# Attention over 1,024 keys and values: one unit of probabilities in eight turned by TensorE, where it was one in four

## What is computed

```python
def _L2_xattn_ref(x, cond, Wq, bq, Wkv, bkv, Wp, bp):
    ...
    q = (x @ Wq + bq).reshape(1, B * N, H, hd)
    kv = (cond @ Wkv + bkv).reshape(1, -1, 2, H, hd)
    ...
    attn = jnp.einsum('bhqd,bhkd->bhqk', q, k)
    attn = jax.nn.softmax(attn.astype(jnp.float32), axis=-1)
    attn = _fq_unsigned(attn, axis=-1)      # s = max/255; round(x/s) clipped to 0..255, times s
    out = jnp.einsum('bhqk,bhkd->bhqd', attn, v)
    out = jnp.transpose(out, (0, 2, 1, 3)).reshape(B, N, C)
    return out @ Wp + bp
```

## Time and profile before

| | us |
|---|---|
| median of three runs | 1028.89 (1026.59 to 1029.68) |
| the profiled execution | 1028.76 |
| its span, first to last instruction | 1027.0 |
| the attention loop, first maximum to the last exponentials (578.65 to 773.75) | 195.1 |
| TensorE, VectorE, ScalarE busy in that stretch | 140.6, 165.2, 173.2 |
| granted TensorE clock over the span, and in that stretch | 0.844, 0.51 |

### The profile page before, as it was taken

How to read it: one execution, slowest core, us unless ns; L and a number is a source line. 1 busy time by engine, 2 the same in 40 slices (tenths; PEclk the granted TensorE clock), 3 DMA queues, 4 the chain that set the end, 5 groups by cost and what they waited for, 6 DMA issues and landing times.

```text
span 1027.0 us, 11627 instructions
## 1 busy us (share of the span) xinstructions
PE 858.3 (84%) x4214; PEld 508.3 (49%) x4214; DVE 728.5 (71%) x958; ACT 461.2 (45%) x695; POOL 166.3 (16%) x251
## 2 busy tenths in 40 slices
PE   5989974589799999989899677677778988879898
PEld 3434652345655555545455333343344656644566
DVE  1776669954558787887668888788884456568767
ACT  2214436731424422212124588899995444622211
POOL 1000000000022442326100261111110100001412
PEclk9899995589889999989899855555558899979999
DMA  8602003000123221340104889967761000000000
GB/s 257 202 1 47 1 0 63 6 3 6 29 37 45 39 37 16 63 56 4 31 16 76 160 156 158 159 124 137 138 128 32 31 0 1 1 1 1 10 11 21
DMA packets 211613, 59.14 MB, mean 58 GB/s; under 512 B 192399, under 2 KB 209893, under 8 KB 211557
## 3 DMA queue, kind: packets, MB, share of 16 engines
q1 hardware_dynamic: 211444, 58.23, 29.2%
q10 hardware_dynamic: 112, 0.17, 0.1%
HBM read 20.62 MB, written 1.05 MB: 21 GB/s over the span
## 4 chain that ended last, share of the span: by engine, by line
PE 51%; DVE 27%; ACT 9%; issue 6%; DMA 5%; POOL 1%; ACTq 1%; DVEq 0%; POOLq 0%
PE ps L950 48%; DMA arena<-xc 4%; DVE arena L2609 4%; ACT xc L1893 2%; ACT arena L1903 1%; DVE arena L2243 1%; DVE arena L2173 1%; PE ps L1081 1%; DVE xc L2415 1%; ACT arena_split L1810 1%; DVE arena L2618 1%; DVE sq L2522 1%; DVE sq L2519 1%; PE ps L472 1%; DVE arena L2157 1%
## 5 line engine op out<-in xcount | busy, mean ns | idle before, releaser
L950 PE MATMUL ps<-arena 128*128 128x16 f16 (+7 forms) x1760 | 268.5, 324 | 62.2 <-ACT xc L1893 27.1
L950 PEld LDWEIGHTS ps<-arena 128*128 128x128 f16 (+4 forms) x1760 | 132.1, 129 | 172.9 <-issue 81.7
L950 PE MATMUL ps<-arena_split 128*128 128x512 f32 (+6 forms) x736 | 197.9, 432 | 18.7 <-DVE arena_split L2065 5.8
L950 PEld LDWEIGHTS ps<-arena_split 128*128 128x128 f32 (+6 forms) x736 | 133.3, 194 | 90.0 <-issue 40.5
L2609 DVE TENSOR_REDUCE arena<-ps 128x1 f32<-128x1024 f32 x128 | 152.4, 1220 | 29.8 <-PE ps L950 28.1
L1893 ACT ACTIVATE xc<-ps,arena 128x1024 int16<-128x1024 f32 x128 | 153.2, 1202 | 21.9 <-POOL arena L908 18.8
L950 PE MATMUL ps<-sq,arena 128*64 128x256 f32 (+3 forms) x256 | 80.9, 515 | 8.1 <-DVE sq L2522 8.1
L908 POOL TENSOR_SCALAR arena<-arena 128x1 f32<-128x1 f32 x128 | 33.8, 264 | 192.9 <-DVE arena L2609 192.6
L857 POOL TENSOR_SCALAR arena<-arena 128x512 f32<-128x512 f32 x12 | 23.1, 1921 | 249.0 <-DVE arena L2437 249.0
L1662 ACT ACTIVATE act_buf<-ps 128x512 f32<-128x512 f32 (+2 forms) x34 | 20.3, 597 | 90.5 <-PE ps L950 90.4
L950 PE MATMUL ps<-mean_w,sq 128*128 128x1 f32 x240 | 34.4, 273 | 21.3 <-ACT sq L1627 21.3
(11 more groups left out here) (291 smaller groups left out, 1322.0 us busy)
## 6 DMA issues: line engine op xcount, KB each, us to landing
arena<-in_L_ffn_w SPq DMA_DIRECT2D x4, 640.0 KB, 6.1
arena_split<-arena_split SPq DMA_DIRECT2D x59, 32.0 KB
arena<-xc SPq DMA_TRANSPOSE x96, 3.3
arena<-in_x SPq DMA_DIRECT2D x1, 1024.0 KB, 6.2
arena<-in_ctx SPq DMA_DIRECT2D x1, 1024.0 KB, 8.7
arena<-in_L_xattn_Wkv SPq DMA_DIRECT2D x2, 512.0 KB, 4.1
arena<-in_L_ffn_gate_w SPq DMA_DIRECT2D x1, 1024.0 KB, 10.0
arena<-in_L_ffn_up_w SPq DMA_DIRECT2D x1, 1024.0 KB, 12.5
```

The source lines that it names most:

```text
L950: return pe.matmul(o, l, r, start=start, stop=stop)
```

## The change

One unit of eight (u % 8 == 7) is turned by TensorE, not two. Unit 3 of each eight becomes a DMA transpose on SP's queue with a semaphore of its own. VectorE copies what TensorE turns; ScalarE's 16 copies (L1903) are gone. The copy waits in the units named change accordingly (u // 8 + 1 in place of u // 4 + 1, unit u-8 in place of u-4 as the previous user of bank 7).

```diff
-        att_copied_dve, att_copied_act = sem("att_copied_dve"), sem("att_copied_act")
-        att_t = {i: sem(f"att_t{i}") for i in range(8) if i % 4 != 3}
+        att_copied = sem("att_copied")
+        att_t = {i: sem(f"att_t{i}") for i in range(7)}
...
         def by_pe(u):
 
-            return u % 4 == 3
-
-        def copied_by_act(u):
-
             return u % 8 == 7
...
         def turned_back(u):
 
             if by_pe(u):
-                return (att_copied_act if copied_by_act(u) else att_copied_dve), u // 8 + 1
+                return att_copied, u // 8 + 1
             return att_t[u % 8], 16 * (u // 8 + 1)
...
             def probs_turned(u):
                 pe.wait_ge(att_exp, u + 1)
-                if u >= 4:
-
-                    pe.wait_ge(*turned_back(u - 4))
+                if u >= 8:
+
+                    pe.wait_ge(*turned_back(u - 8))
...
-            for u in range(UNITS + 4):
-                if u < UNITS:
-                    exponentials(u)
-                if u >= 4 and copied_by_act(u - 4):
-                    probs_copy(u - 4)
+            for u in range(UNITS):
+                exponentials(u)
...
-                if u >= 4 and by_pe(u - 4) and not copied_by_act(u - 4):
+                if u >= 4 and by_pe(u - 4):
                     probs_copy(u - 4)
```

More of the change, by code:

```diff
@@ L625, in probs_read @@
         def probs_read(u):
-            return (att_pe_turned, u // 4 + 1) if by_pe(u) else (att_t[u % 8], 16 * (u // 8 + 1))
+            return (att_pe_turned, u // 8 + 1) if by_pe(u) else (att_t[u % 8], 16 * (u // 8 + 1))
         def turned_back(u):
             if by_pe(u):
-                return (att_copied_act if copied_by_act(u) else att_copied_dve), u // 8 + 1
+                return att_copied, u // 8 + 1
             return att_t[u % 8], 16 * (u // 8 + 1)
@@ L2612, in probs_copy @@
             def probs_copy(u):
-                dve.wait_ge(att_pe_turned, u // 4 + 1)
+                dve.wait_ge(att_pe_turned, u // 8 + 1)
                 if u >= 8:
@@ L2618, in probs_copy @@
                 dve.tensor_copy(att_yt[:, u % 8].rearrange("p a b -> p (a b)"), ps[:, 7, :].bitcast(I16)
-                                ).then_inc(att_copied_dve, 1)
+                                ).then_inc(att_copied, 1)
             def out_copied(h, banks):
```

## The result

| | before | after |
|---|---|---|
| median | 1029.41 us (1026.59 to 1034.89), 12 runs | 1027.06 us (1022.68 to 1028.73), 12 runs |
| ratio | | 0.9967, 95% interval 0.9953 to 0.9981 |
| profiled execution: span | 1027.0 | 1025.6 |
| the exponentials' starts, first to last | 192.2 | 187.4 |
| all outside of that | 834.8 | 838.2 |

The kernel became 0.33% faster, 3.4 us by the ratio, where 9.2 us were forecast. The time lies inside the range, but the gain is a third of the one foretold. So the question is where the other 6 us went.

A forecast was written before the change was run, and what follows sets the result against it. No engine was full; rings of waits with hardly any slack set the attention loop's pace. A gain of 18.3 us, less 2.0 and (8.4 + 2.1 - 3.4), left 9.2: from 1028.76 to 1019.6 us, range 1012.5 to 1028.5.

The forecast's parts named there:

- The copies' 1.29 us a period: Attention loop: without ScalarE's copy, its 0.91 us and the 0.38 behind it fall away every eight units.
- One turn goes, one stays: no gain booked: Attention loop: of TensorE's two turns per eight units one goes, without gain; the remaining one costs what the other did.
- The price of a turn: Attention loop: the remaining TensorE turn, with VectorE's copy, makes two slow steps between exponentials, 1.70 and 1.73 us.
- The quiet period, 10.75: Eight undisturbed units of the attention loop: 10.62 us plus 0.13 for taking out a tile, against 11.90 before.
- The query tiles, 8.4: Four query tiles on SP's queue in the loop delay the units behind them: 2.1 us each, 8.4 in all.
- DMA backlog and slow landings, 2.0 + 2.1: Loop's DMA transposes: 2.0 us for lateness within runs of units, 2.1 for two of four other slow landings.
- The sign that I had named: ScalarE's waits move from the bias to the DMA, concentrated behind the four query tiles, 8 to 10 us in sum.
- Rival 1: DMA in the loop is hidden altogether, only the query tiles cost what they did: 1013.5 us; chance 0.16.
- rival 2: Loop's runs of seven transposes land after about 4.5 us, not 3.3, eating the gain: 1028 us; chance 0.13.
- Rival 3: Loop's exponentials wait for DMA transposes, which become the bound; kernel slower, 1043 us, or 1035 at 4.8 landing; chance 0.09.
- the page's figure: Loop's DMA transposes at 261 GB/s, not 192: a unit passes in 1.0 us, query tiles cheaper, sum near 1016.
- The preference for TensorE: For a 128 x 128 transpose the page prefers TensorE, the DMA taking over three times as long; against the change.

The follow-up runs named there:

- b_dve: The kernel before with both copies on VectorE, one unit in four still turned by TensorE: 1019.83 us, ratio 0.9902 to the kernel before.
- a_noq: The changed kernel with the transposes of the loop's four query tiles left out (output wrong, time only): 1019.08 us, ratio 0.9896 to the kernel before.
- a_buf7: The changed kernel with seven buffers for the probabilities in place of four: 1016.10 us, ratio 0.9862 to the kernel before.

## Why the prediction was wrong, point by point

Two terms of the sum were too small. What late landings cost apart from the query tiles was put at 2.0 + 2.1 = 4.1 us and measured 6.1, because the slow landings are 11 or 12 fetches of instructions and not four accidents, and the faster ring no longer covers them. The quiet period was put at 10.75 and measured 10.87, which is 1.9 us in the loop. Together they are about 4 of the 6 us that are missing; the rest lies outside the loop.

**The copies' 1.29 us a period.** Right in kind: freeing ScalarE is the whole gain. b_dve shows the period fall by 1.03 with nothing else changed. It is not the 1.29 itself, for the step of 2.10 goes to 1.73, where VectorE's copy now stands, and the step behind the other turn falls from 1.70 to 1.24.

**"One turn goes, one stays: no gain booked."** Right in its number, and partly by luck: b_dve and the changed kernel have the same period within 0.02, but the same arithmetic gave b_dve 11.6, and what holds its period is VectorE without a break. What I did not draw from it is that the half that fills the DMA queue then buys nothing, and is to be charged for all that it costs. I made one sum of both halves, where a sum for each would have shown it.

**The price of a turn.** The step I put at 1.70 is 1.71 and 1.55 by turns in the changed kernel, 1.71 in both kinds of period without `tile_out`, and 1.24 in b_dve, for which I expected a period of 11.6 and found 10.89. So it held for the changed kernel and not for another order of the ring. That it depends on the lead that the steps before it leave is argued, as said above.

**The quiet period, 10.75.** Measured 10.87. Half of the miss is the period without a tile, 10.68 for 10.62; the other half is the tile, 0.19 a period for 0.13 (0.37 a tile for 0.26). Over 15.9 periods the miss is 1.9 us.

**The query tiles, 8.4.** 8.7 by a_noq. Right.

**DMA backlog and slow landings, 2.0 + 2.1.** Measured 6.1, what is late in a_noq. I had taken the slow landings for rare accidents, four in the loop, two of them exposed. They are fetches of instructions, 11 or 12 in a loop. Eight of 12 delayed units in the kernel before and eight of 11 in the changed one: they were as frequent before, and the copy's slack was their cover. The sign that I had named shows it: ScalarE's waits for the DMA are 19.7 us in sum, not 8 to 10. The earlier trace rows was one of them, and I did not ask what else was on the DMA engines then.

Together: forecast for the loop 192.2 - 9.2 = 183.0; with 1.9 more for the period and 2.3 for lateness (14.8 in place of 12.5) it comes to 187.2, and the traces show 187.4 and 187.3. So in the loop 4 to 5 us were gained, and 3.4 and 2.6 by the ratios; the difference lies outside the loop, and its cause is open.

**The rivals.** Rival 1, a DMA hidden altogether, is out by the same 19.7 us. The outcome is rival 2 in size, with another mechanism. The median landing stayed at 3.3, so runs of seven do not land at 4.5; single groups do, and a ring with hardly any slack pays for them. Rival 3 can be dropped: the DMA engines were at 0.96 and still not the bound, as a_buf7 passes the same bytes in 178.3 us.

**Rate and engine.** The rate is as the earlier trace rows had it: 169 GB/s over the loop and about 200 while units pass, below the 261 GB/s of the Trainium skill's "DMA: Bandwidth & Descriptors", and the cheaper query tiles that follow from the page's figure are not in the trace. The preference for TensorE in the Trainium skill's "VectorE: DVE Perf Modes" ("Rules for kernel authors") came out right in this kernel: of the two kernels with equal periods, b_dve, with more turns by TensorE, was 7 us faster than the changed one (1019.83 against 1027.06).

## What to carry to other kernels

When a change does two things, make a sum for each: here one half alone was worth 10 us, the other alone nothing, and on top of the first it cost 7, so that together they looked like a small success. A wait of ScalarE that is 0.1 us short of mattering is not hidden; ask of every ring of buffers how much lateness it can take, and count the events that make things late (other transfers on the same queue, fetches of instructions) before the ring is sped up, since the slack that goes away was their cover. And when a ring gets more buffers, look for the next one: three more buffers of 2 KB a partition were worth 11 us in the changed kernel, 10 in b_dve and 3 in the kernel before, and what was late then was waited for by TensorE.

## What the runs showed of the hardware

- DMA transposes in flight were held up while a 16 KB block of instructions was fetched. In the case shown throughput fell from about 200 GB/s to nothing for 0.7 us and to about 10 for 0.8 us more, and the three units in flight landed after 4.3 to 5.0 us, not 3.3; over the traces of before and after the late ones took 3.9 to 5.5 us. Such a fetch came about every 16 us in this loop (11 or 12 in 190 us), and with half of the value matmuls every 25 us (7 from 583 to 758). Eight of 12 of them met transposes that then landed late.
- A 256 KB transpose holds SP's queue for 1.28 us and lands after a median of 3.3 us, in runs of three (before) as in runs of seven (changed), where the DMA engines' share is 0.96. By its place in a run of seven the median is 3.2 to 3.4 us.
- The same program's parts before and behind the loop differed by up to 5 and 7 us between two executions (585.1 and 580.3, 247.9 and 254.5), and behind the loop the granted clock differed too (0.95 and 0.93). The loop, in which the clock stays at its lower level (0.50), repeated within 1 us.
